# A fused decoder layer on one core: cross keys projected once for a pair of heads and doubled by transfers, one weight copy moved

## The reference

```python
x = x + self_attention(layernorm(x))    # q = s Wq + bq, tq = q A, softmax(q tq^T / 16) v, all 256 wide, s = row-normalised input
x = x + cross_attention(layernorm(x), ctx)  # 4 heads of 64: k, v = ctx Wkv; softmax(q k^T / 8) v; Wo
x = x + experts(layernorm(x))           # 4 experts, one chosen for each row by argmax; W1, exact gelu, W2 (256 -> 1024 -> 256)
```

## Time and profile before

| what | us |
|---|---|
| median of 3 runs | 825.46 (823.55 to 825.78) |
| the profiled execution: its own time | 823.08 |
| the profiled execution: span, first to last instruction | 821.3 |
| PE busy | 759.4 (92%) |
| DVE busy | 628.6 (77%) |
| ACT busy | 457.8 (56%) |
| POOL busy | 165.5 (20%) |

### The profile page before, as it was taken

One profiled execution on the slowest core, in us unless ns is written; L12 is line 12 of the kernel. 1 busy time (PEld: TensorE's weight loads), 2 busy tenths in 40 slices (PEclk: granted clock), 3 DMA queues, 4 the chain that ended last, 5 costly groups with the idle time before them and its releaser, 6 DMA issues. The chain is left out here.

```text
span 821.3 us, 19989 instructions
## 1 busy us (share of the span) xinstructions
PE 759.4 (92%) x6226; PEld 684.1 (83%) x6227; DVE 628.6 (77%) x1608; ACT 457.8 (56%) x930; POOL 165.5 (20%) x254
## 2 busy tenths in 40 slices
PE   3978889999999999999999999999998769999996
PEld 2768779989888898888988889888897658999996
DVE  5983747888888888888888888888886755777773
ACT  2544636666666666666666666666664622444342
POOL 3100130212303123031230312303122011222221
PEclk9999999999999999999999999999998959999999
DMA  6232243314223141231412313123169381111110
GB/s 218 72 116 98 72 135 110 103 39 134 65 74 106 38 132 59 80 106 38 132 60 78 106 38 130 63 76 106 38 218 415 123 326 27 36 41 39 40 33 15
DMA packets 51143, 80.90 MB, mean 99 GB/s; under 512 B 4894, under 2 KB 29216, under 8 KB 50976
## 3 DMA queue, kind: packets, MB, share of 16 engines
q1 hardware_dynamic: 49232, 75.63, 27.5%
q0 software_dynamic: 1872, 4.76, 1.6%
HBM read 45.60 MB, written 35.18 MB: 98 GB/s over the span
## 5 line engine op out<-in xcount | busy, mean ns | idle before, releaser
L1134 ACT ACTIVATE ps_cross<-flip 128x512 f16<-128x512 f32 (+1 forms) x256 | 124.8, 515 | 111.2 <-PE flip L846 90.1
L1359 DVE TENSOR_TENSOR ps_cross<-flip,ps_cross 128x512 f16<-128x512 f32 (+1 forms) x256 | 144.9, 583 | 31.6 <-ACT ps_cross L1134 30.0
L1320 ACT ACTIVATE exp_cross<-exp_cross,xneg 128x1024 f32<-128x1024 f32 (+1 forms) x128 | 122.7, 960 | 26.9 <-DVE xneg L1519 26.9
L846 PE MATMUL flip<-ident,exp_cross 128*128 128x128 f32 (+1 forms) x832 | 130.9, 280 | 6.7 <-DVE ps_cross L1359 3.3
L835 PE MATMUL scores<-keys_cross,qt 128*128 128x402 f32 x512 | 125.7, 367 | 2.7 <-ACT exp_self L1309 1.9
L723 PE MATMUL scores<-keys_self,u_tile 128*128 128x512 f32 x384 | 102.4, 404 | 6.3 <-issue 4.6
L846 PEld LDWEIGHTS flip<-ident,exp_cross 128*128 128x128 f32 (+1 forms) x832 | 95.1, 142 | 14.7 <-DVE ps_cross L1359 5.0
L822 PE MATMUL flip<-vals_self,ps_self 128*128 128x256 f32 x768 | 103.0, 288 | 0.0
L857 PE MATMUL cross_out<-vals_cross,ps_cross 128*128 128x128 f16 (+1 forms) x832 | 102.0, 224 | 0.2
L822 PEld LDWEIGHTS flip<-vals_self,ps_self 128*128 128x128 f32 x768 | 96.2, 193 | 0.0
L859 PE MATMUL cross_out<-vals_cross,ps_cross 128*128 128x64 f16 (+1 forms) x832 | 95.2, 195 | 0.0
(11 more groups left out here) (199 smaller groups left out, 1241.8 us busy)
## 6 DMA issues: line engine op xcount, KB each, us to landing
rows_dram<-pads SPq DMA_DIRECT2D x17, 520.0 KB, 3.9
w_piece<-W SPq DMA_DIRECT2D x32, 256.0 KB, 2.9
w_dram<-w_high SPq DMA_DIRECT2D x32, 256.0 KB, 2.3
w_dram<-w_piece SPq DMA_DIRECT2D x32, 256.0 KB, 2.7
w1s<-w_dram SPq DMA_DIRECT2D x8, 1024.0 KB, 13.6
w2s<-w_dram SPq DMA_DIRECT2D x8, 1024.0 KB, 11.4
u_dram<-u_out SPq DMA_DIRECT2D x4, 1024.0 KB, 5.9
u_tile<-u_dram SPq DMA_DIRECT2D x16, 256.0 KB, 2.7
```

Source lines behind the costliest of these rows:

```text
L846: tr = pe.transpose(flip[0:rows, bank(use), n * P:(n + 1) * P], exp_cross[:, h % 2, m * P:m * P + rows], ident[:, :])
L1134: return act.activation(out, in_, ACT.Copy, **kw)
L1320: act.activation(exp_cross[:, h % 2, cols], exp_cross[:, h % 2, cols], ACT.Exp, bias=xneg[:, h % 2, 1:2], scale=-1.0, accum_out=xden[:, ha ...
L1359: return dve.tensor_tensor(out, full, hi, ALU.subtract)
```

## The change

**Keys.** `wk_dup` becomes `wk_cross`, the plain weights, 256 columns in two parts. For each group of 402 context rows there are now two products instead of four: each takes 128 columns, so a pair of heads, and gives the even head's keys on partitions 0 to 63 and the odd head's on 64 to 127. ACT and DVE write both to the place of the even head. SP then sets what is missing with transfers inside SBUF. `odd_keys(n)` copies the odd head's keys from the upper partitions of the even head's place to both halves of its own, two transfers for each of eight products. When all sixteen have landed, `even_keys` copies the even heads' keys from the lower to the upper half, over what the odd ones left there, in four transfers. PE waits for these (`keys_doubled`) ahead of the first cross scores. In SP's queue all of it stands between `loads_x(0)` and the wait for `prologue_done`.

**Maxima.** The largest absolute values of `v_f32` are taken chunk by chunk, 13 reductions, ahead of DVE's wait for `u_stored`. The scale is made after the second key product instead of after the eighth, and the scaled values follow each key from the third on.

**Piece.** For tile 0 alone `piece_high` moves on ACT from between the copies of xt and q to behind `self_hi(j, k, 3)`, the copy of the last flipped part of the exponentials.

```diff
@@ SP
+        def odd_keys(n):
+            sp.wait_ge(cross_k_hi, n + 1)
+            sp.wait_ge(cross_k_lo, n + 1)
+            cols, h = slice((n // 2) * KB, (n // 2 + 1) * KB), 2 * (n % 2)
+            for half in (slice(HD, P), slice(0, HD)):
+                sp.dma_start(keys_cross[half, :, h + 1, cols].bitcast(F32), keys_cross[HD:P, :, h, cols].bitcast(F32)).then_inc(odd_keys_set, 16)
+
+        def even_keys(h):
+            for part in range(2):
+                sp.dma_start(keys_cross[HD:P, part, h, :].bitcast(F32), keys_cross[0:HD, part, h, :].bitcast(F32)).then_inc(keys_doubled, 16)
...
         loads_a(0)
         loads_x(0)
+        for n in range(8):
+            odd_keys(n)
+        sp.wait_ge(odd_keys_set, 16 * 16)
+        even_keys(0)
+        even_keys(2)
 
         sp.wait_ge(prologue_done, 3)
@@ POOL
-        pool.wait_ge(v_max_part, 4)
+        pool.wait_ge(v_max_part, MC)
@@ PE
         for g in range(4):
-            for h in range(H):
-                if g:
-                    pe.wait_ge(cross_k_lo, H * (g - 1) + h + 1)
-                elif h < 2:
+            for pair in range(2):
+                n = 2 * g + pair
+                if n >= 4:
+                    pe.wait_ge(cross_k_lo, n - 3)
+                elif n < 2:
                     pe.wait_ge(pro_q_lo, C * GROUPS)
                 else:
                     pe.wait_ge(pro_v_biased, 4 * GROUPS)
-                three(scores[:, h, 0:KB], lambda a, c: wk_dup[:, a, c, h, :, :],
+                three(scores[:, n % 4, 0:KB], lambda a, c: wk_cross[:, a, c, pair * P:(pair + 1) * P],
                       lambda b, c: ctx_t[:, b, c, g * KB:(g + 1) * KB]).then_inc(cross_k_ready, 1)
...
-        pe.wait_ge(cross_k_lo, 4 * H)
+        pe.wait_ge(cross_k_lo, 8)
...
             if h == 0 and half == 0:
+                if k == 1:
+                    pe.wait_ge(keys_doubled, 16 * 4)
@@ ACT
-                for dup in range(2):
-                    copy(wk_dup[:, 0, :, :, dup, :], w2_raw[:, 0, :, :].rearrange("p c (h d) -> p c h d", h=H)).then_inc(cross_w_hi, 1)
-                for n, w in ((1, wv_cross), (2, wq_cross), (3, wo_cross)):
+                for n, w in ((0, wk_cross), (1, wv_cross), (2, wq_cross), (3, wo_cross)):
...
+        for n in range(8):
+            act.wait_ge(cross_k_ready, n + 1)
+            copy(keys_cross[:, 0, 2 * (n % 2), (n // 2) * KB:(n // 2 + 1) * KB], scores[:, n % 4, 0:KB]).then_inc(cross_k_hi, 1)
+            if n >= 2:
+                values_hi(n - 2)
+        values_hi(6)
+        values_hi(7)
...
-            if a:
+            if a and k >= 1:
                 piece_high(j)
...
             if a:
                 self_hi(j, k, 3)
+            if k == 0:
+                piece_high(j)
@@ DVE
+        for m in range(MC):
+            dve.wait_ge(cross_v_copied, m + 1)
+            dve.tensor_reduce(v_max[:, 0, m:m + 1], v_f32[:, m, :], AX.X, ALU.max, apply_absolute_value=True).then_inc(v_max_part, 1)
...
         dve.wait_ge(u_stored, 16 * GROUPS)
+        for n in range(8):
+            dve.wait_ge(cross_k_hi, n + 1)
+            cols = slice((n // 2) * KB, (n // 2 + 1) * KB)
+            low(keys_cross[:, 1, 2 * (n % 2), cols], scores[:, n % 4, 0:KB],
+                keys_cross[:, 0, 2 * (n % 2), cols].bitcast(F32)).then_inc(cross_k_lo, 1)
...
+            if n >= 2:
+                values_lo(n - 2)
+        values_lo(6)
+        values_lo(7)
```

More of the change, by code:

```diff
@@ L179, in emit @@
     w2_raw = sb("w2_raw", [P, 4, C, D], F32, pro2)
-    wk_dup = sb("wk_dup", [P, 2, C, H, 2, HD], F32R, pro2)
+    wk_cross = sb("wk_cross", [P, 2, C, D], F32R, pro2)
     wv_cross = sb("wv_cross", [P, 2, C, D], F32R, pro2)
@@ L184, in emit @@
     v_f32 = sb("v_f32", [P, MC, D], F32, pro2)
-    v_max = sb("v_max", [P, 2, 4], F32, pro2)
+    v_max = sb("v_max", [P, 2, MC], F32, pro2)
     v_top = sb("v_top", [P, 2], F32, pro2)
@@ L275, in emit @@
     v_max_part = sem("v_max_part")
+    odd_keys_set = sem("odd_keys_set")
+    keys_doubled = sem("keys_doubled")
     v_top_ready = sem("v_top_ready")
@@ L1190, in _, with values_hi @@
         act.wait_ge(pro_v_lo, 4 * GROUPS)
[L1191 to L1199, removed]
+        def values_hi(n):
+            for m in value_chunks(n):
+                act.wait_ge(v_scale_step, 4)
+                act.activation(vals_cross[:, m, :, 0, :], v_f32[:, m, :].rearrange("p (h d) -> p h d", h=H), ACT.Copy,
+                               scale=v_scale[:, 0:1]).then_inc(cross_v_hi, 1)
+        for n in range(8):
[5 more added lines that the diff above has]
+        values_hi(7)
         copy(barrier[:, 0:1], ident[:, 0:1]).then_inc(prologue_done, 1)
@@ L1443, in _ @@
             if g == 0:
[L1444 to L1450, removed]
+                dve.wait_ge(cross_w_hi, 1)
+                low(wk_cross[:, 1, :, :], w2_raw[:, 0, :, :], wk_cross[:, 0, :, :].bitcast(F32)).then_inc(cross_w_lo, 1)
             if g == 1:
                 for n, w in ((1, wv_cross), (2, wq_cross), (3, wo_cross)):
-                    dve.wait_ge(cross_w_hi, 2 + n)
+                    dve.wait_ge(cross_w_hi, 1 + n)
                     low(w[:, 1, :, :], w2_raw[:, n, :, :], w[:, 0, :, :].bitcast(F32)).then_inc(cross_w_lo, 1)
@@ L1457, in _ @@
             low(ctx_t[:, 1, :, cols], ctx_raw[:, :, 0:min(KB, M - g * KB)], ctx_t[:, 0, :, cols].bitcast(F32)).then_inc(ctx_lo, 1)
-        dve.wait_ge(u_stored, 16 * GROUPS)
[L1462 to L1486, removed]
@@ new lines, in _, with values_lo @@
+        for m in range(MC):
+            dve.wait_ge(cross_v_copied, m + 1)
+            dve.tensor_reduce(v_max[:, 0, m:m + 1], v_f32[:, m, :], AX.X, ALU.max, apply_absolute_value=True).then_inc(v_max_part, 1)
+        def values_lo(n):
+            for m in value_chunks(n):
+                dve.wait_ge(cross_v_hi, m + 1)
+                dve.wait_ge(v_scale_step, 4)
+                dve.scalar_tensor_tensor(out=vals_cross[:, m, :, 1, :], in0=v_f32[:, m, :].rearrange("p (h d) -> p h d", h=H),
+                                         scalar=v_scale[:, 0:1], in1=vals_cross[:, m, :, 0, :], op0=ALU.mult,
+                                         op1=ALU.subtract).then_inc(cross_v_lo, 1)
@@ new lines, in _ @@
+        dve.wait_ge(u_stored, 16 * GROUPS)
+        for n in range(8):
[3 more added lines that the diff above has]
+                keys_cross[:, 0, 2 * (n % 2), cols].bitcast(F32)).then_inc(cross_k_lo, 1)
+            if n == 1:
+                dve.wait_ge(v_pool_step, 2)
+                dve.tensor_reduce(v_top[:, 0:1], v_max[:, 1, :], AX.X, ALU.max).then_inc(v_top_ready, 1)
+                dve.wait_ge(v_top_ready, 1)
+                dve.tensor_scalar(v_top[:, 1:2], v_top[:, 0:1], 1e-30, 1.0 / V_TOP, ALU.max, ALU.mult).then_inc(v_scale_step, 1)
+                dve.wait_ge(v_scale_step, 2)
+                dve.tensor_copy(v_scale[:, 1:2], v_top[:, 1:2]).then_inc(v_scale_step, 1)
+                dve.reciprocal(v_scale[:, 0:1], v_top[:, 1:2]).then_inc(v_scale_step, 1)
+            if n >= 2:
+                values_lo(n - 2)
@@ L1487, in _ @@
+        values_lo(6)
+        values_lo(7)
         dve.wait_ge(cross_v_lo, MC)
-        dve.wait_ge(cross_k_lo, 4 * H)
+        dve.wait_ge(cross_k_lo, 8)
         dve.tensor_copy(barrier[:, 1:2], ident[:, 0:1]).then_inc(prologue_done, 2)
```

## The result

The changed kernel takes 832.34 us, the median of 6 runs (829.71 to 834.01), against 824.79 (823.55 to 827.24) for six runs of the kernel before beside it. The ratio is 1.0085 [1.0069, 1.0102]: slower, by 7.5 us. The profiled execution has 831.83 us, its span 830.0.

The account below looks back on a forecast made before the run. PE bounds the steady tiles; at the start a chain through tile 0's and 1's weight pieces decides. Of the engines' 9.5 us gain 0.1 is left, against 1.1 for the clock: +1.0, 826.4 us; range just under 820.2 to just under 831.3.

Parts of the forecast that it names:

- 82.2 + 12p: SP's queue: landing time of tile 0's weight piece behind the twenty key transfers; 106.2 forecast, against ACT having it at 100.56 before.
- p: SP's queue: data time of 412 kB, a pair of odd transfers or one even; taken as 2.0 us, bounds 1.0 and 2.4.
- a charge for the clock: PE idle ahead of tile 1's cross scores: one drop to the 1.2 GHz level, 1.1 us, bounds 0 and 2.2.
- The rival with ctx_raw's row: Key transfers at ctx_raw's rate, p = 2.4: tile 1's piece lands at 123.0, time 831.3, slower; chance 0.15.
- Mask and piece: End of the queue before tile 0's piece lands: 0.73 MB at 408 GB/s, 1.8 us, plus 0.6 to landing.
- DVE's low parts: Prologue weights: DVE makes one low part instead of four, 0.7 us less, so PE's key projection starts at 74.7.
- The engines' part: Prologue up to tile 0's scores: they start 9.5 us earlier, the gain if left to the engines alone.
- The reduction over partitions: POOL's reduction for v_scale, now 13 columns: 2.4 us and no wait; at 3.6 everything on the engines 1.3 us later.
- The chain from the piece: Tile 0's piece to tile 1's: copy 1.06, subtraction 2.37, then 8.5 us for stores and load; landing at 118.2.
- The configuration on POOL: Ahead of POOL's first subtraction: lasts 7.8 us, comes 8.5 us earlier, past at 98.6, so hidden.
- Full rate: Rival, key transfers at 408 GB/s, p = 1.0: piece lands at about 96, 5.3 us faster, 820.2; chance 0.27.
- The chain does not bind: Rival, tile 1's piece or stores go quicker, or POOL's reduction waits: 1 to 2 us either way, 824 to 828; chance 0.13.

## Why the prediction was wrong, step by step

**The step that failed** is the landing of tile 0's piece, "82.2 + 12p. For p = 2.0 that is 106.2". It landed at 111.4, 5.2 later. By terms: first data of the odd transfers at 79.7 instead of 78.2, 1.5; the odd transfers 18.4 us instead of 16.0, 2.4; the pause as predicted, 1.6; the even ones 8.2 instead of 8.0, 0.2; mask and piece to the landing 3.5 instead of 2.4, 1.1. The mechanism was right, and the terms of the queue were too small. Of the 6.5 us between the forecast (+1.0) and the measurement (+7.5), 5.3 are there at tile 1's piece (123.54, forecast 118.2), 0.5 are a charge for the clock that was too small, and 0.7 came later and were not followed. The terms of the landing:

- *Rate.* The forecast of p was nearly right: 412 kB at 187 to 207 GB/s are 2.0 to 2.2 us. The rival with ctx_raw's row (2.4) gave the wrong reason for a nearly right time: its 831.3 lies nearest to what came, but through a slower rate, which did not occur. That is luck.
- *Company.* I left out POOL's four transfers of pads (4 x 130 KB, issued from 89.46 on). In the kernel before they go out at 96.59, with the mask and the piece, and together these 1.26 MB take until 100.5 (308 GB/s at a DMA share of 0.92 from 96.5 on). Now the barrier opens them while the odd transfers run: in 18.4 us there are 3.29 MB of keys and 0.53 of pads. With 2.1 us for a pair, 0.1 more than I took, the eight pairs make 0.8 of the 2.4, and some 1.6 are left for the pads (an estimate from these windows).
- *Mask and piece.* I counted 0.73 MB at 408 GB/s, with nothing beside them and their issues at nothing. Two things came in between, and the runs don't part them. Tile 1's u (0.26 MB) is issued at 107.75 and lands at 112.1, so its data move with the piece's, which they did not before (issued at 100.52, when the piece had landed); and the rate was lower, 158 GB/s at a share of 0.90 from 109 to 110, for a reason that stays open. The issues were longer too, 1.93 and 1.99 us instead of 0.33 to 0.45, and the second half of the piece was issued at 107.21 only. That this cost time is not shown: the even keys' data kept the DMA engines busy until about 107.6, and from 108 to 110 their share is 0.97.
- *Start.* The first data came 1.5 us later; 1.1 of it is the projection's start (75.84, not 74.7). This is not the change: in the eight profiled executions of kernels with the new prologue the projection starts between 74.52 and 76.42, in the three with the old one between 74.69 and 76.08. The 0.7 us that I counted for DVE's low parts can't be told from that. A granted clock of 0.70 from 20 to 25 us, which this execution has, is no cause: the one at 0.66 there starts at 74.64. What makes the spread is open.

**What held.** The engines' part, 8.3 us of the 9.5; the missing 1.2 is this start. The reduction over partitions cost nothing: v_top at 79.28, DVE without a wait for it. The chain from the piece: copy to the end of POOL's subtraction 3.5 us, from there to tile 1's piece 8.6, forecast 3.5 and 8.5; the kernel with the moved copy alone shows that it binds once the piece is late. The configuration on POOL was hidden. PE stood still ahead of tile 1's cross scores, and its clock fell to 0.50. Clock and gaps cost more than the 1.1 us charged: 0.46 by the exponential (the flips of q take 1.08 us, and 0.63 before) and 1.1 from there to the twelve matmuls (6.51 against 5.39), so 1.6, inside the bounds of 0 to 2.2.

**The sum as it came:** 5.2 for tile 1's piece against the kernel before and 1.6 for the clock and the gaps are 6.8 us at the twelve matmuls; 7.5 by the medians. Between the two profiled executions the difference grows further, to 7.9 at tile 15's last cross scores (656.98 against 649.08) and 8.7 at the end of the span; what those last parts are I did not follow, and a single pair of executions can't tell them from scatter.

**The rivals.** *Full rate* is refuted by 187 to 207 GB/s, and the kernel with wide transfers shows that its price was nearly right: I gave 5.3 us faster (820.2), 4.0 came (821.62 against 825.62). *The chain does not bind* is refuted for the changed kernel by SP's last wait, which is for the stores, and by the moved copy alone; in the kernel before, where another wait ended last, it lay some 0.4 us off the bound. My range ended just under 831.3 because I took 2.4 us for a pair as the upper bound of the queue, and did not bound the other traffic of that time.

## What to carry to other kernels

An order of transfers on one queue is part of the critical path even if nobody waits for the transfers themselves: look at what stands behind them, add their data and all other traffic of the time, whichever engine issues it, and only then say that a copy is hidden. A copy between halves of the partitions moves half of what the DMA engines can; twenty of them cost some 11 us here, more than eight projections on PE saved. Look also at every wait that stands between a freed buffer and the next load on the queue: in the kernel before, two of them ended some 0.4 us apart, and which one binds changed from kernel to kernel. Where such a chain bounds the start of a pipeline, work removed ahead of it on the engines is worth only what the chain lets through: 3.9 of 9.3 us without the transfers, 6.3 with the copy back in its place, nothing behind the full queue.

## What the runs showed of the hardware

- Transfers that read one half of the partitions and write one half: 187 to 207 GB/s at a DMA share of 0.94 to 1.00; the same bytes over all 128: 367 to 379, at 1.01 to 1.03.
- An issue of mask, weights or u on SP takes 0.33 to 0.50 us, and 1 to 2 us when transfers are queued up (sixteen over 17.29 us, 1.93 and 1.99 for mask and piece). That is not the only cause: a store at 129.55 took 1.76 us in the changed kernel, at a DMA share of 0.17 from 127 to 130.
- POOL's configuration ahead of its first subtraction costs 6.9 to 7.8 us when the piece is early (7.78 in the earlier trace rows; 7.21, 7.33 and 6.85 in the kernels with the copy in its old place and an early piece) and nothing when it is late (the idle time is then ended by ACT's copy). In these four executions it runs on from the instruction before it, not from the wait.
- After 4.08 us without work PE was at half clock for 8 us, in which it was busy for 6.45.
